# Layernorm of two of four batches done with channels on the partitions, instead of turned on TensorE

## The reference

```python
xn = _layernorm(x, axis=-1)
s = _L0_attn_ref(xn, wq, wk, wv, wo)      # 16 query heads, 4 key/value heads of 128, rope, decay
g = _silu(_L0_ffn_ref(xn, gate_w, up_w, down_w, gate_scale, up_scale, down_scale))   # 512 -> 1536 -> 512
x = x + s * g
```

```python
def _layernorm(x, axis=-1, eps=1e-05):
    m = jnp.mean(x, axis=axis, keepdims=True)
    v = jnp.var(x, axis=axis, keepdims=True)
    return (x - m) / jnp.sqrt(v + eps)
```

## Time and profile before

| | |
|---|---|
| Median of 3 runs | 910.53 us (909.95 to 910.64) |
| The profiled execution | 909.1 us |
| Its span, first to last instruction | 907.3 us |
| TensorE busy | 890.6 us, 98% |
| DVE, ACT, POOL busy | 634.6, 421.8, 367.1 us |
| DMA packets, moved | 51115, 138.55 MB |

### The profile page before, as it was taken

How to read it: one execution, slowest core, us unless ns; L and a number is a source line. 1 busy time by engine, 2 the same in 40 slices (tenths; PEclk the granted TensorE clock), 3 DMA queues, 4 the chain that set the end, 5 groups by cost and what they waited for, 6 DMA issues and landing times.

```text
span 907.3 us, 12407 instructions
## 1 busy us (share of the span) xinstructions
PE 890.6 (98%) x4104; PEld 738.4 (81%) x4104; DVE 634.6 (70%) x905; ACT 421.8 (46%) x709; POOL 367.1 (40%) x271
## 2 busy tenths in 40 slices
PE   5999999999999999999999999999999999999997
PEld 4888888888888887888888888888888888888886
DVE  7878652676653256766787867678767678788796
ACT  3643443443433446344455444464554545634541
POOL 1011112122122474535456455355454563553544
PEclk9999999999999999999999999999999999999999
DMA  6792304378850524413333413145243043265482
GB/s 212 228 360 108 104 13 161 140 256 311 298 204 10 209 92 143 170 33 154 138 117 140 183 61 140 62 151 204 81 162 129 33 178 142 97 232 163 150 265 71
DMA packets 51115, 138.55 MB, mean 153 GB/s; under 512 B 4224, under 2 KB 25344, under 8 KB 45696
## 3 DMA queue, kind: packets, MB, share of 16 engines
q1 hardware_dynamic: 51072, 138.00, 43.1%
HBM read 96.04 MB, written 41.94 MB: 152 GB/s over the span
## 4 chain that ended last, share of the span: by engine, by line
PE 66%; issue 17%; POOL 13%; DVE 2%; ACT 1%; DMA 0%; POOLq 0%; SPq 0%; DVEq 0%; ACTq 0%
PE bank L1226 65%; POOL d_r L1174 8%; POOL rot L1183 5%; PE bank L1273 1%; DMA stage<-in_x_nat 0%; DVE d_sb L1004 0%; ACT gout L540 0%; PE bank L1382 0%; DVE d_sb L1050 0%; DVE tail_sb L1084 0%; DVE tail_sb L1086 0%; POOL fsplit L1155 0%; DVE acc L1080 0%; DVE rot L990 0%; DVE stats L763 0%
## 5 line engine op out<-in xcount | busy, mean ns | idle before, releaser
L1226 PE MATMUL bank<-xn,aw 128*128 128x512 f32 x960 | 228.6, 389 | 0.0
L1183 POOL TENSOR_TENSOR rot<-rot 128x512 f32<-128x512 f32 x80 | 127.0, 1588 | 237.5 <-DVE rot L991 237.5
L1226 PEld LDWEIGHTS bank<-xn,aw 128*128 128x128 f32 x960 | 179.3, 188 | 36.6
L1226 PE MATMUL bank<-o_r,ow 128*128 128x512 f32 (+1 forms) x792 | 186.1, 385 | 0.0
L1174 POOL TENSOR_TENSOR d_r<-d_sb,d_r 128x512 fp32r<-128x512 f32 x128 | 167.4, 1335 | 38.9 <-ACT d_r L684 38.9
L1226 PE MATMUL bank<-xn,gu_w 128*128 128x512 f32 x768 | 179.9, 389 | 0.0
L1226 PEld LDWEIGHTS bank<-xn,gu_w 128*128 128x128 f32 x768 | 144.2, 188 | 30.1
L1226 PEld LDWEIGHTS bank<-o_r,ow 128*128 128x128 f32 x792 | 144.4, 188 | 28.5
L990 DVE TENSOR_TENSOR rot<-bank,rope 128x512 f32<-128x512 f32 x80 | 55.1, 689 | 94.8 <-ACT rot L664 94.5
L684 ACT CAST d_r<-d_sb 128x512 fp32r<-128x512 f32 x128 | 79.0, 621 | 86.2 <-DVE d_sb L1050 65.3
L663 ACT COPY rot<-bank 64x512 f32<-64x512 f32 x80 | 46.7, 584 | 144.8 <-PE bank L1226 144.3
(11 more groups left out here) (77 smaller groups left out, 942.9 us busy)
## 6 DMA issues: line engine op xcount, KB each, us to landing
xn<-xn_split SPq DMA_DIRECT2D x15, 2048.0 KB, 7.7
v_decayed<-vd_split SPq DMA_DIRECT2D x32, 512.0 KB, 3.6
vd_r<-v_decayed SPq DMA_DIRECT2D x16, 1024.0 KB, 7.1
v_r<-v_split SPq DMA_DIRECT2D x16, 512.0 KB, 5.9
wst<-in_mlp_w SPq DMA_DIRECT2D x10, 768.0 KB, 5.3
xn_split<-xn SPq DMA_DIRECT2D x3, 2048.0 KB, 10.8
stage<-in_attn_w SPq DMA_DIRECT2D x4, 1280.0 KB, 5.7
stage<-in_x_nat SPq DMA_DIRECT2D x16, 256.0 KB, 4.4
```

Source lines behind the costliest of these rows:

```text
L1183: pool.tensor_tensor(rot1[:, r % RRING, :], rot1[:, r % RRING, :], rot2[:, r % RRING, :], ALU.add).then_inc(qk_sum, 1)
L1226: last = pe.matmul(dst, a, b, start=start and x == 0, stop=stop and x == len(pairs) - 1)
```

## The change

For s = 2 and s = 3 the turned copy of x, which the input holds as well (x_t, used at the end of the kernel before), is loaded into four slots of `stage`: channels on the partitions, 512 tokens along a row. In this layout mean and 1/std differ along the row and are the same on all partitions, so they must be rows on every partition. `load_rows` stores the 4 columns of the means and the 4 of 1/std to DRAM (512 elements of 4 bytes each, two DMAs), loads x_t (four DMAs of 256 KB), waits for the stores, and loads the two rows broadcast to 128 partitions (two DMAs of 256 KB) into gout. DVE then subtracts and multiplies (`norm_t`, 8 operations of 128x512 a batch), ACT rounds (`norm_t_hi`, 4 a batch) and DVE takes the remainder (`norm_t_lo`, 4 a batch). x with tokens on the partitions is still loaded for the statistics.

```diff
+            def load_rows(s):
+                sp.wait_ge(rstd_d, s + 2)
+                i0, i1 = s * TT, s * TT + TT
+                sp.dma_start(row_dram[s - 2, 0].rearrange("t p -> p t"), mv[:, i0:i1, 0], allow_slow_non_contiguous=True).then_inc(row_out, 16)
+                sp.dma_start(row_dram[s - 2, 1].rearrange("t p -> p t"), rstd[:, i0:i1], allow_slow_non_contiguous=True).then_inc(row_out, 16)
+                for k in range(KT):
...
+                    sp.dma_start(stage[:, TURNED[s][k], :], x_t[k, :, bass.ts(ORDER[s], S)]).then_inc(xt_in[k], 16)
...
+                sp.wait_ge(row_out, 32 * (s - 1))
+                for r in range(2):
+                    row = row_dram[s - 2, r].rearrange("t p -> (t p)")
+                    sp.dma_start(rows[:, r, :], row.unsqueeze(0).broadcast_to([P, S])).then_inc(row_in, 16)
...
             for m in range(6, MT):
                 load_w(m)
+            load_rows(2)
...
+                    if s == 2 and m == 2:
+                        load_rows(3)
...
             # ACT
+            def norm_t_hi(s, k):
+                act.wait_ge(scaled, (s - 2) * KT + k + 1)
...
+                act.copy(xn_of(s)[:, 0, k, :], stage[:, TURNED[s][k], :]).then_inc(ln_hi, 1)
...
-                    if s == 2 and m in (2, 3):
-                        norm(3 * TT + 2 * (m - 2))
-                        norm(3 * TT + 2 * (m - 2) + 1)
-                    if s == 2 and LND <= m < LND + TT:
-                        norm_hi(3 * TT + m - LND)
+                    if s == 2 and m in (5, 6):
+                        norm_t_hi(3, 2 * (m - 5))
+                        norm_t_hi(3, 2 * (m - 5) + 1)
...
             # DVE
+            def norm_t(s, ks):
+                dve.wait_ge(row_in, 32 * (s - 1))
...
+                    dve.tensor_tensor(xt, xt, rows[:, 0, :], ALU.subtract).then_inc(centred, 1)
...
+                    dve.tensor_tensor(xt, xt, rows[:, 1, :], ALU.mult).then_inc(scaled, 1)
+            def norm_t_lo(s, k):
+                dve.wait_ge(ln_hi, s * TT + k + 1)
+                dve.tensor_tensor(xn_of(s)[:, 1, k, :], stage[:, TURNED[s][k], :], xn_of(s)[:, 0, k, :].bitcast(F32),
+                                  ALU.subtract).then_inc(ln_lo, 1)
...
-                if 7 <= m < 7 + TT:
-                    norm_lo(2 * TT + m - 7)
+                if m in (MT - 2, MT - 1):
+                    norm_t(2, (2 * (m - MT + 2), 2 * (m - MT + 2) + 1))
+                if m == MT - 1:
+                    norm_t_lo(2, 0)
+                    norm_t_lo(2, 1)
                 fuse(1, m)
+            norm_t_lo(2, 2)
+            norm_t_lo(2, 3)
...
-                    if s == 2 and LND <= m < LND + TT:
-                        norm_lo(3 * TT + m - LND)
+                    if s == 2 and m in (5, 6):
+                        norm_t(3, (2 * (m - 5), 2 * (m - 5) + 1))
+                    if s == 2 and m in (6, 7):
+                        norm_t_lo(3, 2 * (m - 6))
+                        norm_t_lo(3, 2 * (m - 6) + 1)
...
             # TensorE
-                if 7 <= m < 7 + TT:
-                    ln_transpose(2 * TT + m - 7)
...
-                    if s == 2 and LND <= m < LND + TT:
-                        ln_transpose(3 * TT + m - LND)
```

More of the change, by code:

```diff
@@ L67 @@
 SPILL = 4
-LND = 4
+NAT = [i % XRING for i in range(3 * TT)] + [4, 5, 0, 1]
+TURNED = {2: [0, 1, 2, 3], 3: [2, 3, 4, 5]}
 DECAY_JOBS = [(2, 0), (2, 1), (0, 0), (0, 1), (1, 0), (1, 1), (3, 0), (3, 1)]
@@ L142, in attention_mlp_kernel @@
         mlp.close()
+        rows = gout[:, 0:2, :]
         wv_raw = f_all[:, MT - KT:MT, :]
@@ L218, in attention_mlp_kernel @@
         floor_c = sem("floor_c"); newton = sem("newton"); rstd_d = sem("rstd_d")
+        row_out = sem("row_out"); row_in = sem("row_in"); xt_in = [sem(f"xt_in{k}") for k in range(KT)]; centred = sem("centred"); scaled = sem("scaled")
         normed = sem("normed"); ln_t = sem("ln_t"); ln_hi = sem("ln_hi"); ln_lo = sem("ln_lo")
@@ L281, in load_x @@
             def load_x(i):
-                if i >= XRING:
-                    sp.wait_ge(ln_t, i - XRING + 1)
-                sp.dma_start(stage[:, i % XRING, :], x_nat[ORDER[i // TT], :, i % TT, :]).then_inc(x_in[i % XRING], 16)
+                if i >= 3 * TT + 2:
+                    sp.wait_ge(ln_lo, 2 * TT + NAT[i] + 1)
+                elif i >= 3 * TT:
+                    sp.wait_ge(stats_d, i - 1)
+                elif i >= XRING:
+                    sp.wait_ge(ln_t, i - XRING + 1)
+                sp.dma_start(stage[:, NAT[i], :], x_nat[ORDER[i // TT], :, i % TT, :]).then_inc(x_in[NAT[i]], 16)
+            def load_rows(s):
[4 more added lines that the diff above has]
+                for k in range(KT):
+                    if s == 2:
+                        sp.wait_ge(ln_t if k < 2 else stats_d, 2 * TT if k < 2 else 2 * TT + k - 1)
+                    else:
+                        sp.wait_ge(ln_lo if k < 2 else stats_d, 2 * TT + k + 3 if k < 2 else 3 * TT + k - 1)
+                    sp.dma_start(stage[:, TURNED[s][k], :], x_t[k, :, bass.ts(ORDER[s], S)]).then_inc(xt_in[k], 16)
+                if s == 2:
+                    for r in range(2):
+                        sp.wait_ge(v_out[r], 32 * (2 * TT // VFIRST))
+                else:
+                    sp.wait_ge(gate_out, 16 * KT)
+                sp.wait_ge(row_out, 32 * (s - 1))
+                for r in range(2):
+                    row = row_dram[s - 2, r].rearrange("t p -> (t p)")
+                    sp.dma_start(rows[:, r, :], row.unsqueeze(0).broadcast_to([P, S])).then_inc(row_in, 16)
             def load_piece(q):
@@ L608, in _ @@
                     w_floor(PARTS * SLABS + m + 2 - SLABS)
-                if m in (6, 7):
-                    norm(2 * TT + 2 * (m - 6))
-                    norm(2 * TT + 2 * (m - 6) + 1)
-                if 7 <= m < 7 + TT:
-                    norm_hi(2 * TT + m - 7)
+                if m in (MT - 2, MT - 1):
+                    norm_t_hi(2, 2 * (m - MT + 2))
+                    norm_t_hi(2, 2 * (m - MT + 2) + 1)
             fuse_hi(MT)
@@ L761, in tile_stats @@
             def tile_stats(i):
-                dve.wait_ge(x_in[i % XRING], 16 * (i // XRING + 1))
-                dve.bn_stats(stats[:, i, :], stage[:, i % XRING, :]).then_inc(stats_d, 1)
+                dve.wait_ge(x_in[NAT[i]], 16 * (NAT[:i].count(NAT[i]) + 1))
+                dve.bn_stats(stats[:, i, :], stage[:, NAT[i], :]).then_inc(stats_d, 1)
             def mean_var(grp):
@@ L1259, in v_tile @@
                     pe.wait_ge(ln_lo, v + TT)
+                    pe.wait_ge(v_lo, v)
                 else:
```

23 lines of the change are left out of this document (14 added, 9 removed).

## The result

| | before | after |
|---|---|---|
| Median (4 runs each) | 910.59 us (909.95 to 911.01) | 921.94 us (921.6 to 922.73) |
| The profiled execution | 909.1 us | 922.73 us |
| Its span | 907.3 us | 920.9 us |
| TensorE busy | 890.6 us | 892.4 us |
| Mean granted clock | 1.000 | 0.994 |

The ratio is 1.0129, 95% interval 1.0117 to 1.014: 11.4 us slower. The forecast was 912.5 with a range of 906.4 to 914.8. The direction was the likelier one, the size lies outside the range.

What follows compares the result with a forecast made beforehand. TensorE bounds the kernel (890.6 of 907.3 us busy), DVE second. Removed turns save 4.0 us, but gates 2.5 us later make the down product 2.0 us later: 910.53 becomes 912.5 us, range 906.4 to 914.8.

Steps and rivals of the forecast that it cites:

- Row transfers: SP before unit 3's stores of s = 2: standing until rows land, between 176 and 180 us, costs 0 to 1.2 us.
- head start: DVE's full stretch from 188 us, set by ACT's rounding at 187.71, starts 1 us sooner, between 0 and 2.
- Slower by more: Rival, chance 0.08: SP held past 180 us or TensorE waiting at 146.5 us; +4.4 to +6, 915 to 916.5 us.
- DVE's debt: DVE, 188 to 209 us: nine more operations add 5.4 us, idle time absorbs 2.1; vd_split pair about 2.5 us later.
- No term below is a change of clock: Whole forecast: granted clock taken as 1.00 in the stretches that matter, so no time was allotted to clock changes.
- The turns: TensorE: eight groups of four turns removed at 0.50 us each, 4.0 us in all, half in each of two stages.
- The other price: TensorE: about 275 ns a turn from the Trainium skill, 8.8 us for 32 turns, kernel ending at 901.7; not adopted.
- The third batch: Batch at 107 to 148 us: new xn ready by 145.1, wanted at 146.5; margin 1.4 us, no wait counted.
- What is late next: End of second stage: ACT's gates end at 234.9 us, TensorE's down product waits for them, 2.0 us later than before.
- small waits may stand before it: TensorE before the first down product of the fourth batch: small waits for ACT's f_all possible, no size given.
- All hidden, faster: Rival, chance 0.20: gates come at least 3.5 us sooner and all 4.0 us are kept, 906.5 us.
- The chain keeps its old time: Rival, chance 0.22: DVE's added work is offset, the down product comes 0.5 us sooner, 910.0 us.

Runs made afterwards that it cites:

- e6: Changed kernel with the change kept for s = 2 only, s = 3 turned on TensorE as before: 908.36 us, ratio 0.9975 to the kernel before.
- e11: Changed kernel without row stores; for s = 3 also no x_t loads, broadcasts, subtractions or multiplications in place of the turns: 908.54 us, ratio 0.9982.
- e1: Changed kernel without the row stores and SP's wait for them, rows broadcast from a row of x instead: 914.2 us, ratio 1.0048.
- e3: Changed kernel with SP's wait and the two broadcasts for s = 3 moved behind unit 4's vd_split stores: 921.16 us, ratio 1.0122.
- e8: Kernel before plus only the two 4-byte-piece row stores in s = 2, nobody waiting for them: 915.91 us, ratio 1.0058.
- e9: Changed kernel without row stores; for s = 3 the subtractions and multiplications also left out, all loads kept: 911.12 us, ratio 1.001.
- e10: Changed kernel without row stores; for s = 3 the x_t loads and broadcasts also left out, subtractions and multiplications kept: 911.62 us, ratio 1.0012.
- e7: Changed kernel with the change for s = 2 only and its rows packed into one store of 128 pieces of 32 bytes: 909.72 us, ratio 0.9993.
- e12: Kernel before plus only one packed store of 128 pieces of 32 bytes in s = 2: 910.67 us, ratio 1.0004.
- e4: Changed kernel with one packed row store of 128 pieces of 32 bytes and one broadcast per batch, DVE reading in 32-byte steps: 919.17 us, ratio 1.0098.

## Why the prediction was wrong, by its own steps

**The account.** To the kernel before: third batch -1.8 (e6); fourth batch's turns 0.0 (e11); the loads in front of unit 3's stores +2.7; DVE's work +3.2, together 0.5 less; row stores +7.7 (after less e1). Sum 11.3 of 11.4 us. The parts are differences of medians that close by the way they are taken; the 7.7 is well clear of noise, each of the smaller ones is sure to about 1 us.

**The step that failed: "Row transfers".** It took the landing of 512 elements of 4 bytes from three rows of other transfers, of 2.5, 4.0 and 5.6 us, as an interval. None of the three has that many small pieces, and an interval between unlike things is no bound. It measured 10.4 and 11.0 us. "SP stands still until the rows have landed, between 176 and 180 us" became 187.09, or 185.55 without the offset, and what was "0 to 1.2 us", inside the head start, is 7.7 us at the end.

**A second path was missing from it.** The step priced only SP's standing. e3 and e8 show that the stores do the harm without any wait on SP, with the DMA engines busy at 0.92 and 107 GB/s ahead of the vd_split stores (e8). The two paths lead to the same place, ACT's rounding, so they do not add up, and curing one is not seen.

**The rival "Slower by more"** named this mechanism, "Row transfers hold SP past 180 us". It had 0.08 and 915 to 916.5 us. Its price carried the delay only as DVE's debt. But a rounding that comes 10.5 us late (197.49, offset 1.54, against 185.49) is not absorbed: ACT takes its instructions in order, so the silu of the next unit stood behind the waiting rounding, and TensorE behind that.

**The clock.** "No term below is a change of clock" was true of the trace before. The waits brought slow products: 3.5 us by their durations. That they cost 3.5 us is not shown, and the traces speak against it. e9 and e1 have the same idle stretch ahead of the same products, with and without the lower level:

```profile
228.21 2.73 PE L1288 MATMUL bank<-xn,gu_w 128*128 128x512 f32 x8 [2.75 <-ACT f_all L563]
```

In e9 eight products take 2.73 us and the twelve for v 3.88 (granted clock 0.86 from 230 to 240 us), and no wait for gout follows. In e1 they take 2.08 and 2.89 (1.00), and TensorE waits 1.53 us for gout. e10, after 2.78 us idle, has 2.06 us and a wait of 1.72. The down product starts behind the gates in all of them. So at this place the slow products fill time in which TensorE would have waited. It is likely at 200.29 too, where a wait of 1.38 us follows for a silu that ACT starts at 208.22, behind roundings that waited 3.04 us for DVE's stage. It also follows that the length of the idle stretch alone does not decide whether slow products come.

**The turns: right.** Periods are 5.44 us in units 4 and 5 and 9.07 us in the first stage (9.56 before), and the boundary came 1.98 us sooner against 2.0 forecast. The other price, 8.8 us for 32 turns by the record's length, would be 4.4 us for the 16 turns of e6, which gave 1.8 us.

**The third batch: right**, no wait at 146.5 us. The margin was smaller than the 1.4 us forecast: DVE's last remainder ends at 147.56 in the kernel after and the first product starts at 148.01, so 0.45 us were left. The forecast had allowed for that: another operation slowed by POOL was to take 1.1 of the 1.4 us. e7 used up what was left.

**DVE's debt: right.** +5.4 - 2.1 = 3.3 us forecast for nine operations, 3.2 measured for eight (e10 less e11). The nearness of the two numbers is partly luck, with 1 us of doubt in the measured one.

**The head start: wrong in size.** I counted ACT's second rounding of unit 4 as 1 us sooner, between 0 and 2. In e9 it is at 188.90 with offset 0.85, so 188.05, 0.3 us later than the 187.71 of before; without the loads, in e11, it is at 186.79 with offset 1.03, 185.8, and has the whole head start. 1.5 MB of loads ahead of the stores took all of it. In e1 this rounding is at 188.45 with offset 0.32, 0.4 us late instead of 1 us early: 1.4 of the 1.6 us by which e1 (+3.6) missed the forecast's +2.0, near the upper end of its own range (914.4).

**What is late next: right in the place** for a kernel without row stores. In e1 the gates start 3.6 us late (233.90, offset 0.32) and the down product waits for gout. The wait before it, for f_all of unit 11, 2.87 us, I had only as "small waits may stand before it". And the rival "All hidden, faster", with all 4.0 us kept, was not to be had in this order: e11, with nothing in the place of the fourth batch's turns, keeps 1.75 us.

**The numbers.** In its last sum the forecast changes two chances over: "All hidden, faster" had 0.20 and "The chain keeps its old time" 0.22, and they are added the other way round. It changes nothing in the result.

## What to carry to other kernels

Before removing work from the engine that is full, ask what paces it a stage later: here one batch's 16 turns gave 1.8 us and the other's nothing, since a chain of stores held the next stage's start with 0.5 us in hand. Look at how a transfer is cut and not only at its bytes: here 2 KB in 512 pieces landed later than 512 KB did. Where the trace has no transfer of that kind, its upper bound is open, and so should be the range. A transfer that nobody waits for can still cost, by what is queued behind it on the same DMA engines: put it where the queue is empty, or pack it, and look at what the packing does to the reader.

## What the runs showed of the hardware that was not expected

- A store of 512 elements of 4 bytes each (2 KB) lands in 10.1 to 11.9 us, at 102 us, where only loads are in flight beside it (10.2 and 11.3 us in e6), as well as at 175 us. In the stretch of 10 us behind two of them the DMA engines are busy at 0.74 to 0.92 and move 69 to 107 GB/s (after, e3, e8). 4 KB in 128 pieces of 32 bytes land in 3.6 to 4.1 us (e12, e4, e7).
- DVE's operations on two fp32 operands of 128x512 take 0.6 us each in a row, and 1.1 us if one operand is read in steps of 32 bytes (e4).
- After an idle stretch of TensorE of 6.79 us the next eight products took 3.65 us instead of 1.97, after one of 1.38 us 2.11. After 2.84 us (after) and 2.75 us (e9) they took 2.79 and 2.73 us, but after 2.87 us (e1) and 2.78 us (e10) 2.08 and 2.06 us. What decides between them stays open.
- The start-up, up to 88 us, varies by 1.7 us between single executions of these kernels.
